# A top-k threshold picked by its rank below a guess, in an attention block on one Trainium2 core

## What is computed

```python
scores = jnp.einsum('bhnd,bhmd->bhnm', q, k) * DHEAD ** (-0.5)
kth = jax.lax.top_k(scores, TOPK)[0][..., -1:]
masked = jnp.where(scores >= kth, scores, jnp.finfo(scores.dtype).min)
attn = jax.nn.softmax(masked, axis=-1)
o = jnp.einsum('bhnm,bhmd->bhnd', attn, v)
```

## Time and profile before

| | |
|---|---|
| median of 3 runs | 6425.28 us |
| the profiled execution | 6424.89 us |
| its span, first to last instruction | 6423.1 us |
| mean granted TensorE clock | 0.802 |
| busy: PE, DVE, ACT, POOL | 73%, 80%, 63%, 23% of the span |
| attention_top | from about 125 us to 4100 us of the span |

### The profile page before, as it was taken

The page is one execution under the profiler, slowest core; times in us unless marked ns, Lnnn a source line. Parts: engine busy times, 40 slices in busy tenths (PEclk is TensorE's granted clock), DMA queues, the critical chain, the costliest instruction groups (busy, mean ns, idle before and its releaser), DMA issues. The chain is left out here.

```text
span 6423.1 us, 124479 instructions
## 1 busy us (share of the span) xinstructions
PE 4659.7 (73%) x37227; PEld 2894.7 (45%) x37227; DVE 5130.3 (80%) x28475; ACT 4074.2 (63%) x5216; POOL 1485.8 (23%) x326
## 2 busy tenths in 40 slices
PE   6565366666666536666666656797699999999999
PEld 3343244443444323434444434443466666666665
DVE  4999999999999999999999999532476667666665
ACT  2675477766777537767777767544166666666665
POOL 0333234433433314433434434200000000000000
PEclk8676677777777657767777767799899999999999
DMA  4000000000000000000000000100301010101012
GB/s 172 5 14 13 4 14 6 14 14 6 14 14 14 5 3 14 14 6 14 14 14 7 14 13 7 45 9 29 141 21 27 20 28 20 28 20 28 20 27 76
DMA packets 79077, 155.57 MB, mean 24 GB/s; under 512 B 8056, under 2 KB 49400, under 8 KB 72440
## 3 DMA queue, kind: packets, MB, share of 16 engines
q1 hardware_dynamic: 78328, 146.72, 7.8%
HBM read 99.50 MB, written 47.19 MB: 23 GB/s over the span
## 5 line engine op out<-in xcount | busy, mean ns | idle before, releaser
L450 POOL TENSOR_TENSOR a_probs<-a_scores,a_probs 128x2304 f32<-128x2304 f32 x288 | 1464.8, 5086 | 2518.2 <-ACT a_probs L395 2518.2
L468 DVE MAX8 a_top<-a_scores 128x8 f32<-128x36 f32 x18432 | 1847.5, 180 | 95.0 <-ACT a_scores L379 41.2
L320 PE MATMUL a_ps_t<-ident,a_probs 128*128 128x128 f32 x5184 | 1097.2, 356 | 950.0 <-ACT a_probs L383 950.0
L320 PEld LDWEIGHTS a_ps_t<-ident,a_probs 128*128 128x128 f32 x5184 | 743.1, 178 | 1211.8 <-ACT a_probs L383 980.9
L390 ACT ACTIVATE a_probs_t<-a_ps_t 128x512 f32<-128x512 f32 (+1 forms) x1440 | 764.9, 554 | 739.8 <-PE a_ps_t L320 714.9
L329 PE MATMUL a_ps_o<-a_probs_t,a_v 128*32 128x128 f32 x10368 | 700.3, 327 | 445.0 <-ACT a_probs_t L390 423.8
L395 ACT ACTIVATE a_probs<-a_scores,a_steep_kth 128x2304 f32<-128x2304 f32 x290 | 640.3, 2208 | 369.0 <-DVE a_minus_max L543 368.7
L941 PE MATMUL b_ps_t<-ident,b_soft 128*128 128x128 f32 x5184 | 826.4, 287 | 24.9 <-issue 24.8
L1009 DVE TENSOR_SCALAR_CACHE_REDUCE b_soft<-b_ps_s 128x2304 f32<-128x2304 f32 x290 | 741.7, 2558 | 79.1 <-PE b_ps_s L928 79.0
L487 DVE MAX8 a_best<-a_top 128x8 f32<-128x216 f32 x2304 | 759.9, 371 | 0.0
L1026 DVE COPY b_soft_t<-b_ps_t 128x512 f32<-128x512 f32 x576 | 371.7, 686 | 470.5 <-PE b_ps_t L941 470.5
(11 more groups left out here) (106 smaller groups left out, 3827.8 us busy)
## 6 DMA issues: line engine op xcount, KB each, us to landing
a_k_stack<-k_parts SPq DMA_DIRECT2D x72, 288.0 KB, 5.9
b_k_stack<-k_parts SPq DMA_DIRECT2D x72, 288.0 KB, 5.9
a_q_ring<-q_parts SPq DMA_DIRECT2D x294, 64.0 KB
b_q_ring<-q_parts SPq DMA_DIRECT2D x294, 64.0 KB
k_parts<-p_high SPq DMA_DIRECT2D x36, 256.0 KB, 2.0
k_parts<-p_rest SPq DMA_DIRECT2D x36, 256.0 KB, 2.0
q_parts<-p_high SPq DMA_DIRECT2D x36, 256.0 KB, 2.0
q_parts<-p_rest SPq DMA_DIRECT2D x36, 256.0 KB, 2.0
```

The lines of the kernel that those rows point to most:

```text
L320: last = pe.transpose(ps_t[(NTG * s + g) % 2][:, P * m:P * m + P], probs[s % 2][:, P * (m0 + m):P * (m0 + m) + P], cst["ident"][:, :])
L450: pool.tensor_tensor(probs[u][:, :], scores_all[:, 2 * (p % 2) + u, :], probs[u][:, :], ALU.subtract).then_inc(masked_ready, 1)
L468: last = dve.max(top8[:, s % 2, c, :], scores_all[:, s % 4, CHUNK * c:CHUNK * c + CHUNK])
```

## The change

The DVE's eight rounds become four. The sums over the chunks' largest and second largest values, weighted, give a guess for each row that lies near the 64th. One instruction per tile counts the candidates at or above the guess, one writes the candidates with those above set to zero (`below`, 216 contiguous values), and four rounds of MAX8 with three of MATCH_REPLACE8 take the 32 largest below the guess. The 64th largest is the one at place 63 minus the count: a product with a 0/1 comparison against the numbers 0 to 31, with an accumulator. Where no place fits, the result is 0 and the row is a doubt of kind 0; kinds 1 and 2 are the two `missed` comparisons, now with >=. A doubt of any kind enters the count of scores above the 64th as before; one of kind 0 first runs the eight rounds over the 216 candidates (rounds_over).

With it the order moves. top8 has two buffers. The marks are signalled at the end of select. PE sums them (now 8 one-column matmuls in place of 2) in tile 1's part, between its first 8 transposes and the scores. ACT's keep_any comes after exponentials(s + 1), no longer before it. The DVE takes both tiles of a pair after another, and does hand_on of the pair before after chunk 28, and invert_sums of the pair two before after chunk 20, of the pair's first tile. The diff, cut to its core (the removed parts of the DVE's code are in the kernel above):

```diff
+WINDOW = 32
+FIRST_GUESS = (0.4404, 0.6478)
...
-            def count_beyond(pair):
-                pe.wait_ge(beyond_ready, pair + 1)
-                for u in range(2):
-                    last = pe.matmul(ps_o[0:1, FLAG_COL:FLAG_COL + 1], beyond[:, u:u + 1], cst["ones"][:, 0:1],
-                                     start=u == 0, stop=u == 1)
-                last.then_inc(beyond_counted, 1)
+            def count_doubts(pair):
+                pe.wait_ge(doubt_ready, pair + 1)
+                for column, kinds in ((FLAG_COL, (0,)), (FLAG_COL + 1, (0, 1, 2))):
+                    marks = [doubt[:, kind, u:u + 1] for kind in kinds for u in range(2)]
+                    for n, mark in enumerate(marks):
+                        last = pe.matmul(ps_o[0:1, column:column + 1], mark, cst["ones"][:, 0:1],
+                                         start=n == 0, stop=n == len(marks) - 1)
+                last.then_inc(doubt_counted, 1)
...
                         turn(s, 0)
                         turn(s, 1)
+                        if u == 1:
+                            count_doubts(pair + 1)
                         score(s + 5, h, tile + u + 5)
...
-                        if u == 0:
-                            count_beyond(pair + 1)
                     add_quadrants(pair)
...
                     for g in range(NTG):
                         keep_turned(s, g, tile)
+                    exponentials(s + 1, tile + 1, parity)
                     keep_any(pair + 1)
-                    exponentials(s + 1, tile + 1, parity)
                     keep_scores(s + 5, tile + 5)
...
-            def select(pair):
+            def select(pair, tops):
                 at["n"] = 0
+                candidates = lambda u: tops[:, u, :, 0:KEEP]
+                below_of = lambda u: below[:, u, :].rearrange("p (c k) -> p c k", k=KEEP)
                 wait_alone(dve, tops_taken, 2 * pair + 2)
+                summed = counted(dve.tensor_reduce(column_sums[:, :, :],
+                                                   tops[:, :, 0:CHUNKS, 0:2].rearrange("p u c k -> p u k c"),
+                                                   AX.X, ALU.add))
...
+                weighted = counted(dve.tensor_scalar(guess[:, :], column_sums[:, :, 0], FIRST_GUESS[0] / CHUNKS, None,
+                                                     ALU.mult))
...
+                guessed = counted(dve.scalar_tensor_tensor(guess[:, :], column_sums[:, :, 1], FIRST_GUESS[1] / CHUNKS,
+                                                           guess[:, :], ALU.mult, ALU.add))
...
+                for u in range(2):
+                    rows = counted(dve.tensor_scalar(below_of(u), candidates(u), guess[:, u:u + 1], None, ALU.is_ge,
+                                                     ALU.add, accum_out=above_guess[:, u:u + 1]))
...
+                for u in range(2):
+                    written[u] = counted(dve.scalar_tensor_tensor(below_of(u), candidates(u), guess[:, u:u + 1],
+                                                                  candidates(u), ALU.is_lt, ALU.mult))
+                counted(dve.tensor_scalar(place[:, :], above_guess[:, :], -1.0, TOPK - 1.0, ALU.mult, ALU.add))
+                for r in range(WINDOW // 8):
...
+                for u in range(2):
+                    after(found[u])
+                    picked_u = counted(dve.scalar_tensor_tensor(picked[:, u, :], places[:, :], place[:, u:u + 1],
+                                                                best[:, u, :], ALU.is_equal, ALU.mult,
+                                                                accum_out=kth[:, u:u + 1]))
+                after(picked_u)
+                counted(dve.tensor_scalar(doubt[:, 0, :], kth[:, :], 0.0, None, ALU.is_le))
+                for n in range(2):
+                    last = dve.tensor_tensor(doubt[:, 1 + n, :], missed[:, n, :], kth[:, :], ALU.is_ge)
+                    counted(last)
+                after(at["n"])
+                dve.sem_clear(dve_order)
+                dve.sem_inc(doubt_ready, 1)
...
+            def rounds_over(array, u):
+                with dve.Fori(0, ROUNDS) as r:
+                    dve.drain()
+                    dve.max(eight[:, :], array)
+                    dve.drain()
+                    dve.match_replace(array, eight[:, :], array, LOWEST)
+                dve.drain()
+                dve.tensor_copy(kth[:, cols(u, 1)], eight[:, 7:8])
...
+                doubtful = dve.value_load(any_doubt[0:1, 1:2], min_val=0, max_val=0x44800000)
                 with dve.If(doubtful > 0):
+                    outside = dve.value_load(any_doubt[0:1, 0:1], min_val=0, max_val=0x44800000)
+                    with dve.If(outside > 0):
+                        for u in range(2):
+                            dve.tensor_copy(scratch[:, 0:(CHUNKS + REST) * KEEP].rearrange("p (c k) -> p c k", k=KEEP),
+                                            top8[parity][:, u, :, 0:KEEP])
+                            rounds_over(scratch[:, 0:(CHUNKS + REST) * KEEP], u)
+                            dve.drain()
...
+            def pair_step(pair, tile, p, before=2):
+                def between(c):
+                    if c == 20 and before > 1:
+                        invert_sums(tile - 4, pair - 2, p % 2)
+                    if c == 28 and before > 0:
+                        hand_on(pair - 1, (p - 1) % 2)
+
+                chunk_tops(tile, 2 * p, between)
                 chunk_tops(tile + 1, 2 * p + 1)
-                select(pair)
...
+                select(pair, top8[p % 2])
```

More of the change, by code:

```diff
@@ L238, in attention_top @@
         scratch = sb("scratch", [P, N])
-        top8 = sb("top8", [P, 2, CHUNKS + REST, 8])
-        best, eight = sb("best", [P, 2, TOPK]), sb("eight", [P, 8])
-        missed, beyond = sb("missed", [P, 2, 2]), sb("beyond", [P, 2])
+        top8 = [sb(f"top8{n}", [P, 2, CHUNKS + REST, 8]) for n in range(2)]
+        below = sb("below", [P, 2, (CHUNKS + REST) * KEEP])
+        best, eight = sb("best", [P, 2, WINDOW]), sb("eight", [P, 8])
+        kth, largest = sb("kth", [P, 2]), sb("largest", [P, 2])
+        column_sums, guess = sb("column_sums", [P, 2, 2]), sb("guess", [P, 2])
+        above_guess, place = sb("above_guess", [P, 2]), sb("place", [P, 2])
+        places, picked = sb("places", [P, WINDOW]), sb("picked", [P, 2, WINDOW])
+        missed, doubt = sb("missed", [P, 2, 2]), sb("doubt", [P, 3, 2])
         flag, flag_t, flags = sb("flag", [P, D]), sb("flag_t", [P, D]), sb("flags", [1, P])
-        any_missed, any_above = sb("any_missed", [1, 1], I32), sb("any_above", [1, 1], I32)
+        any_doubt, any_above = sb("any_doubt", [1, 2], I32), sb("any_above", [1, 1], I32)
         steep_kth = [sb(f"steep_kth{n}", [P, 2]) for n in range(2)]
@@ L467, in chunk_tops @@
                 for c in range(CHUNKS):
[L468 removed]
+                    last = dve.max(top8[s // 2 % 2][:, s % 2, c, :], scores_all[:, s % 4, CHUNK * c:CHUNK * c + CHUNK])
                     if c < CHUNKS - 1:
@@ L477, in select @@
                 written = [0, 0]
+                after(rows)
                 for u in range(2):
[L479 to L483, removed]
+                    written[u] = counted(dve.scalar_tensor_tensor(below_of(u), candidates(u), guess[:, u:u + 1],
+                                                                  candidates(u), ALU.is_lt, ALU.mult))
@@ L571, in _ @@
-            chunk_tops(0, 0)
-            pair_step(0, 0, 0, first=True)
+            for n in range(2):
+                dve.memset(top8[n][:, :, CHUNKS:CHUNKS + REST, 1:KEEP], LOWEST)
+            for n in range(WINDOW):
+                last = dve.memset(places[:, n:n + 1], float(n))
+            last.then_inc(buffers_set, 1)
+            dve.wait_ge(buffers_set, 1)
+            def pair_step(pair, tile, p, before=2):
[5 more added lines that the diff above has]
+                chunk_tops(tile, 2 * p, between)
+                chunk_tops(tile + 1, 2 * p + 1)
+                select(pair, top8[p % 2])
@@ L573, in _ @@
+            for p in range(2):
+                pair_step(p, 2 * p, p, before=p)
             with dve.Fori(0, HEADS - 1) as h:
-                for p in range(1, HEAD_PAIRS + 1):
+                for p in range(2, HEAD_PAIRS + 2):
                     pair_step(h * HEAD_PAIRS + p, h * HEAD_TILES + 2 * p, p)
-            for p in range(1, HEAD_PAIRS):
-                pair_step((HEADS - 1) * HEAD_PAIRS + p, (HEADS - 1) * HEAD_TILES + 2 * p, p,
-                          last=p == HEAD_PAIRS - 1)
@@ L579, in _ @@
-            dve.sem_inc(beyond_ready, 1)
+            for p in range(2, HEAD_PAIRS):
+                pair_step((HEADS - 1) * HEAD_PAIRS + p, (HEADS - 1) * HEAD_TILES + 2 * p, p)
+            invert_sums(HEADS * HEAD_TILES - 4, ALL_PAIRS - 2, 0)
+            hand_on(ALL_PAIRS - 1, 1)
+            dve.wait_ge(any_ready, ALL_PAIRS)
+            dve.sem_inc(doubt_ready, 1)
             dve.wait_ge(penalty_ready, 2 * ALL_PAIRS)
```

61 lines of the change are left out of this document (21 added, 40 removed).

## The result

The changed kernel takes 6903.94 us, the median of 4 runs (6897.53 to 6905.26); the one before 6425.16 beside it. The ratio is 1.0743, with a 95% interval from 1.0724 to 1.0761. The span of the profiled execution is 6901.8 us against 6423.1, 478.7 more, all of it in attention_top.

What follows compares the result with a forecast made beforehand. The loop of ACT and PE was taken to bound the kernel, hiding the DVE's gain. Gate -92 + 347, threshold waits -39, full fallbacks' copies -5, new fallbacks +225: +436 on 6424.9 gives 6861 us, range 6670 to 7010.

Steps and rivals of the forecast that it cites:

- Who sets the pace: A loop of ACT and PE, 24.75 us a pair, paces attention; a shorter DVE loop alone gives 39 us at most.
- The gate, +347 - 92 us: ACT's keep_any waits for PE's transposes and count, 2.41 us a pair (+347); the old wait of 0.64 goes (-92).
- the transposes' 1.37 us: Within the gate: PE's 8 transposes before the count, mean of 1.09, 1.67 and 1.34 us in three pairs.
- the added passes at 0.06 us each: Within the gate: 12 more matmul passes in PE's count, 0.72 us a pair.
- PE's clock, kept at the mixture: PE's granted clock assumed to stay mixed across pairs; all pairs fast or slow would be -210 or +130 us.
- The fallbacks, +225 us: 8 further pairs with a 64th outside the 32 places, 28 us each; rounds over 216 candidates at 1.15 to 1.2 us.
- The DVE's loop of 23.8 us: DVE work per pair, down from 24.7: chunks 12.7, selection 9.8, stop at the threshold 1.3 us.
- the 2 to 3 that I had named as a sign of being right: DVE idle 2 to 3 us a pair around its threshold, waiting for ACT.
- The rival for which the DVE becomes the bound: Dearer dependent small operations make selection 13.5 us and the DVE's loop 27.5, about 7000 us; chance 0.09.
- The 39 us of ordinary waits for the threshold: ACT's waits for the DVE's threshold in the 127 ordinary pairs, 0.3 us a pair, would go: -39 us.
- Rival 2, a gate that is absorbed: ACT's idle time for PE absorbs the gate, the DVE's loop paces: 6430 us with all fallbacks, 6210 with none; "faster" 0.07.

Runs made afterwards that it cites:

- old_select: The changed kernel's order with the kernel before's selection of eight rounds, no guess and no product: 6690 us, 27.15 us an ordinary pair.
- w40_half_pool: w40 with POOL subtracting only half of each row, leaving half of the masking out of the output: 6692 us, 27.21 us a pair.
- fill: The changed kernel with 12 more transposes on PE in the gap before the scores of tile 1: 6781 us, 26.10 us a pair.
- old_fill: old_select with the 12 repeated transposes of fill on PE: 6492 us, 25.63 us a pair.
- old_any_late: old_select with keep_any on ACT behind keep_scores of tile 1: 6648 us, 26.86 us a pair.
- w40: The changed kernel with 40 places instead of 32 and a higher guess, so that no row falls outside: 6897 us, 28.57 us an ordinary pair.
- new_select: The new selection in the order of the kernel before, with the 8 extra fallbacks: 6781 us, 26.34 us an ordinary pair.
- new_fill: The order of the kernel before, the new selection with 40 places, and added transposes keeping PE busy: 6578 us, 26.28 us a pair.

## Why the prediction was right, and where it was off

The forecast of 6860 us in 6670 to 7010 held with 6904, and the mechanism was mostly the one named: a gate in ACT's row, eight more fallbacks, a DVE gain that stays hidden. That the number came so close is in part luck. The gate was priced about 100 us too high, the clock's loss of about 138 us was left out of the sum, and the two nearly cancel. One cause, the stalls behind POOL, was missed.

- **Who sets the pace.** Right for the new order: a DVE that has room doesn't help, old_select and w40_half_pool, with 2.8 and 2.2 us of idle DVE a pair, stay at 27.2 us. For the kernel before it rests on the rows; no run relieves its DVE without bringing in the stalls.
- **The gate, +347 - 92 us.** Right in kind, too large: ACT's wait for the count rose by 154 us, not 255. From the exponential's end to keep_scores were 1.83 us in nearly every pair, not 2.41. Two terms were mis-sized: the transposes' 1.37 us, which were 1.09 in nearly every pair, and the added passes at 0.06 us each. One pass lasts 0.163 us, so 16 in 0.54 us stand (0.54 - 0.163)/15 = 0.025 us apart, and the four in 0.24 us of the earlier trace rows already did: I had divided by four a stretch that holds the last pass's whole length, and so called it nearer the wrong price. The Trainium skill's floor of about 25 ns for a start, cited as the other price from "TensorE: Matmul & The Clock Gate", section "Wait — 56ns, not 53.3ns?", was the nearer one; the trace agrees with its 0.025 us.
- **PE's clock, kept at the mixture.** Wrong. I left it out of the sum with bounds of -210 and +130 us. The granted clock from 1000 to 2000 us fell from 0.72 to 0.64, and the waits for transposed blocks rose by 138 us, a little beyond the upper bound; that the whole 138 are the clock's is argued, not measured. The gap before the scores rose from 0.88 us at most to 2.27, which I had seen and called open. fill and old_fill show that work in this gap brings the clock up; old_any_late, with a gap of 0.42 us and the clock at 0.65, shows that the gap's length alone is not the cause. What lowers the clock in the new order stays open.
- **The fallbacks, +225 us.** Right: eight waits, 203 us. A round over 216 candidates took 0.98 us from MAX8 to MAX8, not 1.15 to 1.2.
- **The DVE's loop of 23.8 us.** Wrong, and nearly fatal to the step that leaned on it. Its work was as priced (9.3 us of selection against 9.8), but 613 us in all went into L500, L504 and L514 standing behind POOL, 4.3 us a pair, so that the loop came to 27.3, level with ACT's, and in ordinary pairs the DVE idled 0.9 us and not the 2 to 3 that I had named as a sign of being right. I had looked at which operations wait for each other and not at what they share with POOL. The Trainium skill states it, in "SBUF — State Buffer", section "Who interferes with whom": a VectorE instruction with two inputs in SBUF contends with a GpSimd instruction that reads SBUF. So does one in a two-port mode, which tensor_scalar without an accumulator can enter, and there whoever issues first holds the shared ports for its whole instruction while the other fully blocks. The trace agrees: these lines reach 4.7 to 5.05 us beside POOL's 5.07, while the selection's MAX8s (0.48 to 0.51 us at 320 elements), its reductions (0.61 to 0.64 at 256) and the scalar form with an accumulator (0.42 to 0.45) hardly vary, and POOL's own subtractions stay at 5.05 to 5.13 us. That L500 runs in the two-port mode is inferred from its stalls.
- **The rival for which the DVE becomes the bound**, given 0.09, was right about the DVE's length and wrong about what causes it. In the changed kernel it cost nearly nothing (ordinary pairs wait 13 us in all for the threshold); it showed when w40 added a round, and in part when fill raised the clock.
- The 39 us of ordinary waits for the threshold went, but for 13.
- **Rival 2, a gate that is absorbed**, was not met: keep_any waits in every pair. Its figures were about 40 us too low by its own terms, as the 39 us of waits are already in its 25.0 us a pair: 6425 - 173 is 6252 with no fallback and 6477 with all of their 225 us, not 6210 and 6430.

What also stays open is the exact length of the pairs in new_select and new_fill: the stall shifts with POOL from pair to pair, and no run here separates its share from the waits it sets off.

## What to carry to other kernels

Before shortening the busiest engine, ask whom the others wait for: here the waits say that the engine at 80% could give back 39 us. Before putting new instructions on VectorE, check which of them have two SBUF inputs or a two-port form and what GpSimd does at that moment; a 2-column multiplication can take 5 us. And a wait put between two stretches of TensorE work can be paid twice, once as itself and once in the granted clock, so read the clock behind it.

## What the runs showed that I had not expected

- Useless transposes in PE's waits made both kernels faster: 0.36% in the kernel before (timed), 123 us in the changed one and 198 us in old_select (one run each).
- VectorE stood still for 613 us behind GpSimd's subtractions, always in the same three lines, two of which work on two columns.
- A 1-column matmul pass costs 25 ns from start to start in a row of 16.
- Cutting PE's gap from 2.27 to 0.42 us left its granted clock where it was (0.65 against 0.64); filling it with work raised it to 0.78.
